# Pair counts on one NeuronCore: a table row of sixteen registers per twelve items on TensorE, one bank wait per four items, eight block ends per tile on ScalarE

## The reference

```python
edge_index = jnp.stack([src, dst])
x = _layernorm(x + _L0_gnn_ref(x, edge_index, ...))       # two ARMA convolutions, batch norms
x = _layernorm(x + _L1_gnn_ref(x, edge_index, W, b))      # GCN, sums over src -> dst with loops
x = _layernorm(x + _L2_gnn_ref(edge_index, edge_type_9, x, ...))  # typed sums, two layers
x = _layernorm(x + _L3_gnn_ref(x, edge_index, ...))       # neighbour sum
# each plain neighbour sum is  out[d] = sum over edges (s -> d) of h[s]
```

## Time and profile before

| what | us |
|---|---|
| median of 3 runs (5015.52 to 5028.06) | 5017.47 |
| the profiled execution, its own time | 5019.42 |
| its span, first to last instruction | 5018.1 |
| first to last multiplication of an item (L1438) in it | 679.0 to 951.2 |

### The profile page before, as it was taken

The page is one execution under the profiler, slowest core; times in us unless marked ns, Lnnn a source line. Parts: engine busy times, 40 slices in busy tenths (PEclk is TensorE's granted clock), DMA queues, the critical chain, the costliest instruction groups (busy, mean ns, idle before and its releaser), DMA issues. The chain is left out here.

```text
span 5018.1 us, 59816 instructions
## 1 busy us (share of the span) xinstructions
PE 3731.9 (74%) x16870; PEld 2393.1 (48%) x16871; DVE 2451.4 (49%) x3832; ACT 960.8 (19%) x2715; POOL 2033.0 (41%) x2229
## 2 busy tenths in 40 slices
PE   5977956598999989999989766666668544444459
PEld 2544522256555535555555555555555433433345
DVE  7989977503888861112235644353436422222221
ACT  2947736414000031111121000000001000000011
POOL 0000000101777711011000577777772777777740
PEclk7978978899999989999989765565558755555569
DMA  0000023543888827356444411111115311111114
GB/s 18 0 0 0 0 79 152 197 114 138 297 293 293 296 73 242 138 177 222 154 175 163 177 52 53 52 54 52 53 53 199 104 52 53 53 53 52 53 59 165
DMA packets 165366, 578.54 MB, mean 115 GB/s; under 512 B 47552, under 2 KB 59425, under 8 KB 164844
## 3 DMA queue, kind: packets, MB, share of 16 engines
q0 software_dynamic: 97200, 308.78, 19.1%
q1 hardware_dynamic: 67638, 267.41, 14.8%
q10 hardware_dynamic: 390, 0.60, 0.0%
HBM read 445.10 MB, written 131.53 MB: 115 GB/s over the span
## 5 line engine op out<-in xcount | busy, mean ns | idle before, releaser
L2113 PE MATMUL ps_sum_rgcn<-gathered_rgcn,select_sum_rgcn 128*128 x3328 | 990.3, 446 | 688.6 <-DMA gathered_rgcn<-by_dst,row 370.6
L2113 PEld LDWEIGHTS ps_sum_rgcn<-gathered_rgcn,select_sum_rgcn 128*128 128x128 f32 x3328 | 772.9, 312 | 764.8 <-issue 760.8
L2028 POOL DMA_INDIRECT gathered_rgcn<-by_dst,row x782 | 740.7, 947 | 238.3 <-issue 233.7
L2028 POOL DMA_INDIRECT gathered_rgcn<-by_src,row x686 | 647.3, 944 | 246.6 <-issue 203.6
L718 PE MATMUL ps_sum_arma<-gathered_sum_arma,select_sum_arma 128*128 128x384 f32 x1664 | 550.1, 491 | 18.6 <-DMA gathered_sum_arma<-arma,other 15.6
L704 POOL DMA_INDIRECT gathered_sum_arma<-arma,other x416 | 393.2, 945 | 375.0 <-POOLq L790 209.5
L1631 PE MATMUL ps_sum_arma<-pair_counts_sum_arma,parts_sum_arma 128*128 128x448 f16 x2625 | 518.8, 353 | 5.0 <-DMA pair_counts_sum_arma<-pairs 5.0
L2182 DVE TENSOR_TENSOR select_sum_rgcn<-one_hot_sum_rgcn,ps_coef_sum_rgcn 128x2048 f32<-128x2048 bf16 x52 | 119.0, 2288 | 679.9 <-PE ps_sum_rgcn L2113 679.8
L718 PEld LDWEIGHTS ps_sum_arma<-gathered_sum_arma,select_sum_arma 128*128 128x128 f32 x1664 | 308.5, 190 | 259.9 <-issue 65.3
L752 DVE TENSOR_TENSOR acc_arma_end<-acc_arma_end,ps_sum_arma 128x768 f32 x416 | 396.9, 954 | 54.0 <-PE ps_sum_arma L718 33.4
L2146 ACT COPY sums_or_hidden_rgcn<-ps_sum_rgcn 128x128 f32<-128x128 f32 x100 | 26.6, 266 | 1867.1 <-PE ps_sum_rgcn L2113 1867.1
(11 more groups left out here) (449 smaller groups left out, 5177.6 us busy)
## 6 DMA issues: line engine op xcount, KB each, us to landing
pair_counts_sum_arma<-pairs SPq DMA_DIRECT2D x125, 800.0 KB, 4.3
by_src<-rows_rgcn_src_table SPq DMA_DIRECT2D x50, 576.0 KB, 2.8
by_dst<-rows_rgcn_dst_table SPq DMA_DIRECT2D x50, 576.0 KB, 3.6
exact<-whole_pairs SPq DMA_DIRECT2D x25, 800.0 KB, 3.4
pairs<-whole_pairs POOLq DMA_DIRECT2D x25, 800.0 KB, 5.1
pair_counts_sum_x<-pairs SPq DMA_DIRECT2D x25, 800.0 KB, 4.5
pair_counts_sum_gcn<-pairs SPq DMA_DIRECT2D x25, 800.0 KB, 4.5
air_counts_sum_neighbour<-pairs SPq DMA_DIRECT2D x25, 800.0 KB, 4.4
```

The source lines that it names most:

```text
L2028: nc.gpsimd.indirect_dma_start(got[:, n % PLACES, :], None, table, bass.IndirectOffsetOnAxis(ap=o.row[:, n % C:n % C + 1], axis=0)).then_i ...
L2113: nc.tensor.matmul(ps[:, bass.ds(slot, P)], select[:, parity, u, :], rows[:, bass.ds(place, D)], start=False, stop=False, skip_group_check ...
```

## The change

PE's table row of sixteen registers now holds twelve bank columns, three bank waits (each that of the fourth item of a four) and a zero, so it serves twelve items. PE loads it 48 times where it loaded 72 times, and it waits on `made` and on `freed` together, once in four items, in one nop. The wait on `freed` asks for the bank of the fourth item before the first of the four starts. The loop has 6 rounds of 96 items where it had 18 of 32. ACT's row of block ends gets an eighth word of padding, so that each tile's row starts at a multiple of eight words; it loads eight registers for seven that it uses. The stage ahead fills the tables in the new layout, with two small memsets more.

```diff
--- before.py
+++ after.py
@@ -1109,6 +1109,9 @@
 
 
 Q_LEAD = 16
+FOUR = 4
+DOZEN = 3 * FOUR
+ROW = 16
 
 
 def spread_stage(nc, k, tag, pairs):
@@ -1256,7 +1259,6 @@
         tile_i = sb("tile_i", [P, ITEMS], I32)
         tile_at = sb("tile_at", [P, ITEMS])
         chunk_at = sb("chunk_at", [P, ITEMS])
-        items = q.item_at[:, :].rearrange("p (n a) -> p n a", a=2)
         ps = c.psum("ps", [P, 8, 512])
         step, numbered, spanned, compared, weighed, taken, summed, spread, flipped, moved, picked, laid = c.sems(
             "step", "numbered", "spanned", "compared", "weighed", "taken", "summed", "spread", "flipped", "moved",
@@ -1319,6 +1321,7 @@
             nc.vector.memset(ones[:, :], 1.0)
             nc.vector.memset(ones_f[:, :], 1.0)
             nc.vector.memset(tile_of[:, C:C + 1], float(NT + 1))
+            nc.vector.memset(q.item_at[:, :, ROW - 1:ROW], 0)
             nc.vector.tensor_scalar(sel[:, :], k.diff[:, 0:1].to_broadcast([P, P]), float(1 - P), None, ALU.is_equal)
             nc.vector.tensor_copy(other[:, :], o.other[:, :])
             for h in range(QUARTERS):
@@ -1366,10 +1369,13 @@
             for h in range(QUARTERS):
                 last_pick = nc.vector.tensor_scalar(pick[:, h, :], chunk_at[0:Q4, :], part_of[0:Q4, h:h + 1], None, ALU.is_equal)
             last_pick.then_inc(picked, 1)
-            nc.vector.tensor_scalar(items[:, :, 1], b_at[:, :], 1.0, None, ALU.add)
+            nc.vector.tensor_scalar(q.item_at[:, :, DOZEN:DOZEN + DOZEN // FOUR],
+                                    b_at[:, :].rearrange("p (n h a) -> p n h a", h=DOZEN // FOUR, a=FOUR)[:, :, :, FOUR - 1],
+                                    1.0, None, ALU.add)
             then(nc.vector.scalar_tensor_tensor(tile_at[:, :], tile_at[:, :], float(-SPANS), b_at[:, :],
                                                 ALU.mult, ALU.add))
-            nc.vector.tensor_scalar(items[:, :, 0], tile_at[:, :], float(SPAN), None, ALU.mult)
+            nc.vector.tensor_scalar(q.item_at[:, :, 0:DOZEN], tile_at[:, :].rearrange("p (n a) -> p n a", a=DOZEN),
+                                    float(SPAN), None, ALU.mult)
             dve.wait_ge(laid, 1)
             for first, w, bank in ((0, SPAN, 1), (SPAN, ITEMS - SPAN, 2)):
                 here = slice(first, first + w)
@@ -1377,7 +1383,9 @@
                                                ALU.mult, ALU.add)
                 nc.vector.tensor_copy(q.source_at[:, here], ps[:, 5 + bank, 0:w])
             dve.wait_ge(spread, 1)
-            nc.vector.tensor_scalar(q.end_of[:, :], ps[:, 3, 0:2 * P], float(Q_LEAD), None, ALU.add)
+            nc.vector.memset(q.end_of[:, :, SPANS:SPANS + 1], 0)
+            nc.vector.tensor_scalar(q.end_of[:, :, 0:SPANS], ps[:, 3, 0:BLOCKS_OF_PAIRS].rearrange("p (t g) -> p t g", g=SPANS),
+                                    float(Q_LEAD), None, ALU.add)
 
 
 def pair_counts_stage(nc, k, q, exact, halves):
@@ -1397,6 +1405,8 @@
         zeroed, made, multiplied, freed, taken, stored0, stored1 = c.sems(
             "zeroed", "made", "multiplied", "freed", "taken", "stored0", "stored1")
         stored, kept = (stored0, stored1), k.kept
+        item_at = q.item_at[:, :, :].rearrange("p n a -> p (n a)")
+        end_of = q.end_of[:, :, :].rearrange("p t g -> p (t g)")
         block = c.block()
 
         def load(engine, table, first, n, top):
@@ -1427,15 +1437,18 @@
             for g in range(SPANS):
                 nc.tensor.matmul(ps[:, g * SPAN:g * SPAN + SPAN], zero16[0:1, 0:P], zero16[0:1, :],
                                  start=True, stop=False, skip_group_check=True)
-            with pe.Fori(0, ITEMS // V // 2) as i:
-                for u in range(2 * V):
-                    if u % 8 == 0:
-                        table = load(PE, q.item_at, i * (4 * V) + 2 * u, 16, (SPANS - 1) * SPAN)
-                    if u % 4 == 0:
-                        pe.wait_ge(made, i * (2 * V) + u + 4)
-                    pe.wait_ge(freed, table[u % 8 * 2 + 1])
-                    nc.tensor.nop(nofuse=True)
-                    nc.tensor.matmul(ps[:, bass.ds(table[u % 8 * 2], SPAN)], source[:, u // V, u % V // 2, :, u % 2],
+            BODY = 2 * DOZEN * V // FOUR
+            with pe.Fori(0, ITEMS // BODY) as i:
+                for u in range(BODY):
+                    if u % DOZEN == 0:
+                        table = load(PE, item_at, i * (BODY // DOZEN * ROW) + u // DOZEN * ROW, ROW,
+                                     (SPANS - 1) * SPAN)
+                    if u % FOUR == 0:
+
+                        pe.wait_ge(made, i * BODY + u + FOUR)
+                        pe.wait_ge(freed, table[DOZEN + u % DOZEN // FOUR])
+                        nc.tensor.nop(nofuse=True)
+                    nc.tensor.matmul(ps[:, bass.ds(table[u % DOZEN], SPAN)], source[:, u // V % 2, u % V // 2, :, u % 2],
                                      target[:, u % V, :], start=False, stop=False, skip_group_check=True).then_inc(multiplied, 1)
 
         @block.scalar
@@ -1450,7 +1463,7 @@
                 nc.scalar.copy(ps[:, here], zero[:, 0:here.stop - here.start]).then_inc(freed, 1)
 
             for i in range(NT):
-                ends = load(mybir.EngineType.Activation, q.end_of, i * SPANS, SPANS, ITEMS + V)
+                ends = load(mybir.EngineType.Activation, end_of, i * (SPANS + 1), SPANS + 1, ITEMS + V)
                 for g in range(SPANS):
                     act.wait_ge(multiplied, ends[g] if i * SPANS + g < BLOCKS_OF_PAIRS - 1 else ITEMS + V)
                     if g == 0 and i >= 2:
@@ -1516,8 +1529,8 @@
         q.target_at = c.sb("target_at", [P, ITEMS])
         q.source_at = c.sb("source_at", [P, ITEMS], FP16)
         q.steps = c.sb("steps", [P, P, 2], FP16)
-        q.item_at = c.sb("item_at", [P, 2 * ITEMS], I32)
-        q.end_of = c.sb("end_of", [P, 2 * P], I32)
+        q.item_at = c.sb("item_at", [P, ITEMS // DOZEN, ROW], I32)
+        q.end_of = c.sb("end_of", [P, NT, SPANS + 1], I32)
         heavy_stage(nc, k)
         staircase_stage(nc, k, q)
         pair_counts_stage(nc, k, q, dram["exact"], dram["pairs"])
```

## The result

| | before | after |
|---|---|---|
| median of 4 runs, us | 5022.23 (5015.52 to 5028.06) | 4946.95 (4940.54 to 4953.86) |
| profiled execution, own time / span, us | 5019.42 / 5018.1 | 4950.41 / 4949.1 |
| first to last item matmul in it, us | 272.2 | 193.7 |

The ratio is 0.9849, with a 95% interval of 0.9832 to 0.9866: 75 us less, where 57 were forecast, inside the range.

The account below looks back on a forecast made before the run. PE's own sequence of matmuls and register-load gaps bounds the 272.2 us stage. Shorter gaps, fewer waits and hidden loads leave PE 206 to 215, middle 210, plus 5 for coupling: 215 us, 57 less, kernel 4960, range 4938 to 4988.

Parts of the forecast that it names:

- (a): PE's gaps at register loads: 24 loads fewer save 23.6 us, at most 32.9; 66 to 75 of 98.6 us left.
- (c): PE's queue runs ahead at the high clock, hiding 0.5 us per load (0.16 to 0.79): 19 us less.
- (b): PE's item matmuls: 432 of 576 waits go, saving 11 us, plus 4 from fewer groups; busy time about 159.
- Rival B: PE's queue does not get ahead at the high clock; stage 225 to 235 us, kernel 4970 to 4980; chance 0.25.
- (d): DVE's work is unchanged, a floor of 192 us for the stage; hindrance between DVE and PE adds 5 us.
- A: Stage as forecast, PE and DVE nearly balanced: 205 to 224 us, kernel 4950 to 4969; chance 0.45.
- C: DVE the only bound, PE's loads vanish under the ring: stage 192 to 203 us, kernel 4937 to 4948; chance 0.12.
- (e): PE's wait on `freed` asks for about one bank more; costed at nothing, at worst 1.0 us per wait.
- (f): ACT's eight aligned registers load faster, about 0.65 us on most of 25 tiles, some 12 us off the bound.
- (g): Loop has 5 back-edges instead of 17: 2.5 us less, part of the gaps already; larger body costs nothing.
- F: Slower because the bank wait bites: at 0.5 us a wait, stage 287 us, kernel 5032; chance 0.04.
- E: Stores and PE loads collide oftener, DMA share 0.47; if half did, kernel 5010; no measurable change, chance 0.05.

Follow-up runs that it names:

- e_wait_only: Kernel before with the bank wait and its nop only once in four items, 72 register loads kept: 5467.44 us, ratio 0.9938 to the kernel before beside it.
- e_loads_only: Changed kernel with the nop and bank wait again on every item, 48 register loads kept: 5468.8 us, ratio 0.9939 to the kernel before beside it.
- half_again: Changed kernel with 17 of 36 source one-hots left out, second run: 4953.37 us, ratio 0.9859 to the kernel before beside it.
- after_third: Changed kernel itself, measured a third time: 4939.86 us, ratio 0.9832 to the kernel before beside it.

## Why the prediction was right, and where it was off

What bounds it: right. PE's own queue was the bound, the loads the gaps, and the releasers that the row named were not: all 98.6 us of idle time ended 0.35 to 0.38 us behind a load. Each part on PE alone shows it.

(a) Gaps: right with (c). 66 to 75 us less 19 is 47 to 56, measured 52.6, nearly all of it at loads. The loads' sum fell by 30.5 us for the 23.6 to 32.9 of the forecast, although their median rose from 1.1 to 1.5 us, where I had left it at 1.1.

(b) This term was mis-sized. Busy time was to fall to 159 us and fell to 141.1. The step of 0.216 us and the groups of 2.76 us came out as forecast; the share of items at the low clock did not. With 576 x 0.216 + 48 x 0.17 = 132.6 us at the high clock and 0.21 more for each item at the low one, 141.1 leaves 8.5 / 0.21 = 40 items, 7%, where I had kept the fifth. The prediction left the clock as it was. It rose with less idle time on PE (0.79 with 121.3 us, 0.87 with 98.6, 0.94 with 52.6), but it does not go by the sum of the idle time: e_wait_only had 0.91 with 84.2 us and e_loads_only 0.88 with 67.5, and on one chip half_again had 0.91 with 55.0 beside after_third's 0.95 with 55.8. What moves it was not tried apart.

(c) Right in its kind, somewhat larger: 0.7 us of a load is hidden for 0.5 taken, from 0.16 to 0.79. Rival B is excluded by the gap of 0.55 us.

(d) The floor of 192 us was right to within 1 us, and the 5 us of hindrance between the two engines were about 2 to 4. So the picture of A held, PE and DVE nearly balanced: DVE idle for 1.1 us where I had 20, PE's queue waiting 6.6 us at most, and neither more work on DVE nor longer loads on PE came free. But the time was C's, 4937 to 4948, to which I had given 0.12. The rest of C did not come true: DVE is not the only bound, and the loads did not vanish. The 206 to 215 for PE by itself held the 18 us too many of (b); less these they are 188 to 197, which is where DVE's 192 stands as well. That term and the smaller hindrance make up the 21 us between the forecast stage of 215 and the measured 193.7.

(e) The bank wait cost little: the 7.1 us of PE's idle time that are put down to cleared banks stand at loads nearly all, and the gaps inside a twelve, four of them, make 1.6 us. It was not tried apart from the rest. (f) ACT's loads fell below the forecast 0.97 us, to 0.55, and are worth next to nothing, as said. (g) Nothing, as said. The rule of the Trainium skill's page "Runtime: NRT & Kernel Launch", section on instruction fetch mechanics, that a taken branch out of the last two blocks of 256 instructions pays a fetch, does not show on TensorE here: back-edges over some 350 and 700 commands took 208 ns at the median or less. (h) Not seen; the time outside the stage scatters by more. F didn't come. The sign that I had set for E did, the median load of PE rose, and the DMA share went to 0.52 where E had 0.47; but only 15 of 48 loads took over 2 us, and E's price did not come. At the mean a load took 1.67 us for 1.53.

## What to carry to other kernels

Where idle time stands ahead of groups of a fixed count, look for what the code does once per that count, before believing the releaser that the row names; here it was a register load. Do so again behind the change: the row of the changed kernel names DVE for 45.4 us that are loads as well. A full engine and no idle time on it do not make it the only bound; here adding work to VectorE and adding load time to TensorE both lengthened the stage by as much as was added. A wait with its nop is not free on an engine's queue, ready or not: it decides whether the queue gets ahead of the array, and so whether the next load is hidden. And a kernel that leaves work out can change something else with it, as the issues of the stores here. When a term at one clock level is carried over to a kernel with fewer gaps, let the clock move too, and give more chance to the rival whose time is the next engine's floor when the sums lie within 10% of each other.

## What the runs showed of the hardware

A register load's time goes by how many registers it fills and where the row begins: 16 aligned ones 1.10 us (TensorE), 8 aligned 0.55 (ScalarE, changed kernel), 7 from a multiple of four words 0.96 to 0.97 (ScalarE, six loads of the kernel before), 7 from elsewhere about 1.63 (its other loads, at the median). With the stores doubled, at a DMA share of 0.64 to 0.84, one on TensorE took up to 3.6 us.

The issue of a store on GpSimd got longer as VectorE got busier. The row of the changed kernel, beside 542 ns at the median in the kernel before:

```profile
L1482 POOL DMA_DIRECT2D pairs<-whole_pairs x25: 531/2448/4573, 687.1 to 872.9; - x25
```

Of its 19 issues over 1 us, 17 end 0.2 us into a `source` one-hot and the other two at one of VectorE's few pauses. One of them began at 789.38 and ended at 793.64, and the `source` one-hot of the rows above began at 793.41:

```profile
L1482 POOL DMA_DIRECT2D pairs<-whole_pairs x1: 4263/4263/4263, 789.4 to 789.4; - x1
```

So here an unbroken run of `target` one-hots held an issue until it ended; with runs twice as long (half_again) one took 8.4 us. The Trainium skill, "DMA: Bandwidth & Descriptors", section "SWDGE vs HWDGE vs iDMA", has it that VectorE in one of its modes locks GpSimd out of the memory in which it writes descriptors, and that DMAs from the hardware queues don't suffer. The numbers agree with that; which mode the `target` one-hots run in no trace tells, and no run here moved the store to another queue.
